# Expert rows stored by slot and gathered by token onto x in SBUF, in place of scatters that add to a copy of x in DRAM

## The reference

```python
# experts are chosen by the token's id; Wg, Wu and Wd are all the context of that expert
def _L0_xattn_ref(hidden_states, token_ids, Wg, Wu, Wd):
    expert_ids = jnp.minimum(tid // tokens_per_expert, E - 1)
    for e in range(E):
        g = jax.nn.silu(jnp.einsum('bsd,fd->bsf', hidden_states, Wg[e]))
        u = jnp.einsum('bsd,fd->bsf', hidden_states, Wu[e])
        y = jnp.einsum('bsf,df->bsd', g * u, Wd[e])
        out = jnp.where((expert_ids == e)[..., None], y, out)
...
x = x + jnp.tanh(g_xattn[0]) * _L0_xattn_ref(_layernorm(x, axis=-1), itok_BxS_13_99985, ctx_2048, ctx_2048, ctx_2048)
x = x + jnp.tanh(g_ffn[0]) * _L0_ffn_ref(_layernorm(x, axis=-1), L0_ffn_w_gate, L0_ffn_w_up, L0_ffn_w_down)
x = x + jnp.tanh(g_xattn[1]) * _L1_xattn_ref(_layernorm(x, axis=-1), ctx_2048, ctx_2048, L1_xattn_gamma)
x = x + jnp.tanh(g_ffn[1]) * _L1_ffn_ref(_layernorm(x, axis=-1), L1_ffn_gate_w, ...)
```

## Time and profile before

| | before |
|---|---|
| median of 3 runs | 1050.43 us (1050.4 to 1052.26) |
| the profiled execution's own time | 1051.51 us |
| its span, first to last instruction | 1049.8 us |
| TensorE busy | 973.2 us, 93% |
| VectorE busy | 632.5 us, 60% |
| ScalarE busy | 420.8 us, 40% |
| GpSimd busy | 639.8 us, 61% |
| mean granted clock of TensorE | 0.979 |

### The profile page before, as it was taken

How to read it: one execution, slowest core, us unless ns; L and a number is a source line. 1 busy time by engine, 2 the same in 40 slices (tenths; PEclk the granted TensorE clock), 3 DMA queues, 4 the chain that set the end, 5 groups by cost and what they waited for, 6 DMA issues and landing times.

```text
span 1049.8 us, 13677 instructions
## 1 busy us (share of the span) xinstructions
PE 973.2 (93%) x4436; PEld 474.9 (45%) x4436; DVE 632.5 (60%) x1168; ACT 420.8 (40%) x817; POOL 639.8 (61%) x565
## 2 busy tenths in 40 slices
PE   6699999969999999799999999999999999999992
PEld 4355555424444444344444445335455555555530
DVE  5478876868888887577777777981222222222221
ACT  4466565434444444466666665332111111111100
POOL 4399996558888887686766661245444554445430
PEclk9899999989999999899999999999999999999996
DMA  9555555240000001230001605178999999999848
GB/s 310 190 131 142 122 144 115 48 143 1 1 1 1 2 1 41 81 130 21 21 23 36 234 1 201 30 259 272 331 336 333 340 335 335 338 335 334 242 63 182
DMA packets 64148, 162.90 MB, mean 155 GB/s; under 512 B 9888, under 2 KB 10032, under 8 KB 63632
## 3 DMA queue, kind: packets, MB, share of 16 engines
q1 hardware_dynamic: 47488, 116.94, 31.9%
q0 software_dynamic: 16464, 40.91, 18.1%
q10 hardware_dynamic: 128, 4.19, 1.2%
HBM read 129.67 MB, written 39.67 MB: 161 GB/s over the span
## 4 chain that ended last, share of the span: by engine, by line
PE 64%; POOL 14%; DVE 8%; issue 7%; DMA 4%; ACT 2%; SPq 0%; POOLq 0%; DVEq 0%; ACTq 0%
PE PS L1580 15%; PE PS L1599 8%; PE PS L1424 6%; PE PS L1401 6%; PE PS L1412 6%; POOL ARENA L665 6%; PE PS L1311 5%; PE PS L1295 5%; POOL ARENA L671 3%; PE PS L1569 3%; PE PS L367 3%; DVE ARENA L986 2%; POOL ARENA L660 1%; DMA XNT<-in_L_ffn_w_down 1%; DVE ARENA L1195 1%
## 5 line engine op out<-in xcount | busy, mean ns | idle before, releaser
L715 POOL TENSOR_TENSOR ARENA<-ARENA 128x512 f32<-128x512 f32 x128 | 133.3, 1063 | 55.8 <-DVE ARENA L1021 55.7
L1366 PE MATMUL PS<-SLAB,ARENA 128*128 128x512 bf16 x512 | 118.8, 382 | 12.6 <-DVE ARENA L972 10.9
L761 POOL DMA_INDIRECT out<-ARENA,idx x32 | 46.2, 1445 | 124.4 <-DVE ARENA L1227 106.8
L1855 ACT ACTIVATE ARENA<-PS 96x192 f32<-96x192 f32 x64 | 20.9, 327 | 226.4 <-PE PS L1580 186.3
L1227 DVE COPY ARENA<-PS 96x512 f32<-96x512 f32 x64 | 41.1, 682 | 94.6 <-PE PS L1599 94.6
L1762 ACT ACTIVATE ARENA<-PS,ARENA 128x512 f32<-128x512 f32 x128 | 86.8, 683 | 23.1 <-DVE ARENA L1015 19.8
L1015 DVE TENSOR_REDUCE ARENA<-PS 128x2 f32<-128x1024 f32 x64 | 78.2, 1222 | 9.3 <-PE PS L1401 9.1
L1366 PEld LDWEIGHTS PS<-SLAB,ARENA 128*128 128x128 bf16 x512 | 48.4, 98 | 75.0 <-issue 21.5
L1580 PE MATMUL PS<-SLAB,ARENA 128*96 128x384 f32 x240 | 81.0, 490 | 0.0
L1412 PEld LDWEIGHTS PS<-ident,ARENA 128*128 128x128 f32 x512 | 54.8, 141 | 51.1 <-issue 36.6
L1728 ACT ACTIVATE ARENA<-PS 128x512 f32<-128x512 f32 x64 | 38.2, 597 | 97.5 <-PE PS L1366 97.5
(11 more groups left out here) (267 smaller groups left out, 1868.3 us busy)
## 6 DMA issues: line engine op xcount, KB each, us to landing
SLAB<-in_L_ffn_w_gate SPq DMA_DIRECT2D x30, 384.0 KB
SLAB<-in_L_ffn_w_up SPq DMA_DIRECT2D x30, 384.0 KB
X<-in_L_ffn_w_down SPq DMA_DIRECT2D x14, 768.0 KB
SLAB<-in_L_ffn_w_down SPq DMA_DIRECT2D x10, 768.0 KB
CT<-in_L_ffn_w_gate SPq DMA_DIRECT2D x16, 384.0 KB
CT<-in_L_ffn_w_up SPq DMA_DIRECT2D x16, 384.0 KB
X<-in_ctx SPq DMA_DIRECT2D x4, 1024.0 KB, 5.5
XNT<-in_L_ffn_w_gate SPq DMA_DIRECT2D x16, 256.0 KB
```

Source lines behind the costliest of these rows:

```text
L715: last = pool.tensor_tensor(prob[s % 4][:, h, :], prob[s % 4][:, h, :], rec[:, s % 4, h:h + 1].to_broadcast([P, D]), ALU.mult)
L1366: last = pe.matmul(bank(b), QT[:, par, k * P:(k + 1) * P], w[:, k, c * D:(c + 1) * D], start=(k == 0), stop=(k == KD - 1))
```

## The change

- The copy `x_sum` is gone, with its four DMAs, the scatters, `target` and `pads`. SP stores each slot's `ysb` to `slot_out` in DRAM, in slot order.
- SP loads x into `X` in SBUF with eight DMAs of two tiles each, in slots 1 to 8.
- When all 19 stores have landed, GpSimd gathers for each token tile i the rows of `slot_out` by `slot[:, i]`, and the DMA adds them to `X` (`gather_x`). Four stand ahead of `deviation_x(0, 1)`, one ahead of `normal_h(0)`, one ahead of `normal_h(1)`, and the other ten in pairs at the end of GpSimd's steps 0 to 4 of the feed-forward.
- `TILED` leaves out slots 6, 12 and 18, and holds all 16 tiles; `REST` is empty. The 15 `unread` multiplications of the passage become 12, in one piece behind y(18).

```diff
         def tile_at(j):
-            return j - (j + 1) // 4
-        TILED = [j for j in range(SLOTS) if j % 4 != 3]
+            return j - j // 6
+        TILED = [j for j in range(SLOTS) if j % 6 or j == 0]
...
+                def store_y(j):
+                    sp.wait_ge(y_out, j + 1)
+                    sp.dma_start(slot_out_v[:, j, :], ysb[:, j % 2, :]).then_inc(y_stored[j % 2], 16)
+
                 for j in range(SLOTS):
                     if j in TILED and tile_at(j) + 2 < NT:
                         load_w(tile_at(j) + 2)
-                sp.wait_ge(y_stored[0], 16 * ((SLOTS + 1) // 2))
-                sp.wait_ge(y_stored[1], 16 * (SLOTS // 2))
-                for i in range(NT):
-                    need(sp, yg_in[i % 4], 16 * (i // 4))
-                    sp.dma_start(X[:, i, :], x_sum_v[:, i, :]).then_inc(yg_in[i % 4], 16)
+                    if 1 <= j <= NT // 2:
+                        need(sp, c_turned, NT)
+                        sp.dma_start(X[:, 2 * j - 2:2 * j, :], x_v[:, 2 * j - 2:2 * j, :]).then_inc(x_in, 16)
+                    if j:
+                        store_y(j - 1)
+                store_y(SLOTS - 1)
...
-                def scatter(j):
-                    if j == 0:
-                        pool.wait_ge(target_ready, 1)
-                        pool.wait_ge(x_in, 64)
-                    pool.wait_ge(y_out, j + 1)
-                    pool.indirect_dma_start(x_sum, bass.IndirectOffsetOnAxis(ap=target[:, j:j + 1], axis=0),
-                                            ysb[:, j % 2, :], None, compute_op=ALU.add).then_inc(y_stored[j % 2], 16)
...
+                def gather_x(i):
+                    need(pool, yg_in[i % 4], 16 * (i // 4))
+                    pool.indirect_dma_start(X[:, i, :], None, slot_out, bass.IndirectOffsetOnAxis(ap=slot[:, i:i + 1], axis=0),
+                                            compute_op=ALU.add).then_inc(yg_in[i % 4], 16)
+
+                pool.wait_ge(x_in, 16 * (NT // 2))
+                pool.wait_ge(y_stored[0], 16 * ((SLOTS + 1) // 2))
+                pool.wait_ge(y_stored[1], 16 * (SLOTS // 2))
+                for i in range(4):
+                    gather_x(i)
                 deviation_x(0, 1)
                 deviation_x(1, 1)
+                gather_x(4)
                 normal_h(0)
                 back_h(0, 0)
                 deviation_x(2, 2)
+                gather_x(5)
                 normal_h(1)
...
                     if live(i, 0):
                         back_i(i, 0, par)
                         normal_i(i, 1, par)
+                    for g in range(2 * i + 6, min(2 * i + 8, NT)):
+                        gather_x(g)
...
-                unread(4)
                 if SLOTS - 1 in TILED:
                     turn_w(tile_at(SLOTS - 1))
-                unread(5)
                 for n in REST:
                     turn_w(n)
-                unread(6)
+                unread(12)
...
-                for b in range(B):
-                    act.dma_start(x_sum[b * S:(b + 1) * S, :], x_rows[b * S:(b + 1) * S, :]).then_inc(x_in, 16)
```

More of the change, by code:

```diff
@@ L102, in build @@
     slot_in = nc.dram_tensor("slot_in", [SLOTS * P, D], F32, kind="Internal").ap()
-    x_sum = nc.dram_tensor("x_sum", [T + SLOTS * P, D], F32, kind="Internal").ap()
+    slot_out = nc.dram_tensor("slot_out", [SLOTS * P, D], F32, kind="Internal").ap()
     rows = nc.dram_tensor("rows", [ROWS, RW], F32, kind="Internal").ap()
@@ L170, in build @@
         hot_ready, counted = sem("hot_ready"), sem("counted")
-        whose_ready, picks_ready, found, token_ready, target_ready = (
-            sem(n) for n in ("whose_ready", "picks_ready", "found", "token_ready", "target_ready"))
+        whose_ready, picks_ready, found, token_ready = (
+            sem(n) for n in ("whose_ready", "picks_ready", "found", "token_ready"))
         h_in = [sem(f"h_in{r}") for r in range(5)]
@@ L202, in build @@
         token = arena(SLOTS, I32)
-        target = arena(SLOTS, I32)
-        pads = arena(2 * SLOTS).rearrange("p (n j) -> p n j", n=2)
         idi = arena(P, I32)
@@ L236, in build @@
         x_rows = x.rearrange("b s d -> (b s) d")
-        x_sum_v = x_sum[0:T, :].rearrange("(i p) d -> p i d", p=P)
+        slot_out_v = slot_out.rearrange("(j p) d -> p j d", p=P)
         def blocks(a, n=BLK):
@@ L629, in _ @@
                         deviation(j + 3)
-                    if j == SLOTS - 1:
-                        scatter(j - 1)
-                    if j in TILED:
+                    if j in TILED and tile_at(j) + 1 < NT:
                         normal(tile_at(j) + 1)
-                    if 0 < j < SLOTS - 1:
-                        scatter(j - 1)
                     if j + HR < SLOTS:
@@ L639, in _ @@
                     normal(n)
-                scatter(SLOTS - 1)
                 def deviation_x(i, n):
@@ L858, in _ @@
                                          op0=ALU.mult, op1=ALU.add).then_inc(token_ready, 1)
[L860 to L865, removed]
                 def top(n):
@@ L925, in _ @@
                     if j in TILED:
-                        scales(n + 1)
+                        if n + 1 < NT:
+                            scales(n + 1)
                         if n + 2 < NT:
@@ L1273, in _ @@
                 for i in range(NT):
-                    last = pe.matmul(bank(3)[:, 0:3 * SLOTS], at_row[:, i, :], picks[:, i].rearrange("p n j -> p (n j)"),
+                    last = pe.matmul(bank(3)[:, 0:2 * SLOTS], at_row[:, i, :], picks[:, i, 0:2].rearrange("p n j -> p (n j)"),
                                      start=(i == 0), stop=(i == NT - 1))
```

## The result

The changed kernel takes **1059.32 us** (median of 4 runs, 1057.37 to 1060.23), beside 1051.35 us for the kernel before (4 runs, 1050.4 to 1052.29). The ratio is 1.0065, with an interval of 1.0052 to 1.0079: slower, by some 8 us in the medians. Six later runs of the same kernel gave 1057.66 beside 1052.72 us, 4.9 us slower (last experiment).

The account below looks back on a forecast made before the run. TensorE was taken to bound the slots, GpSimd and VectorE in turns the feed-forward. -10.2 + 0.2 + 0 + 14.5 = +4.5 on 1051.5 us gave 1056.0, less 1.1 for the median: 1055; range 1043 to 1063.

Parts of the forecast that it names:

- Start of the slots: First layer's early slots: without the copy the weight tile lands in time, z(3) begins at 46.6, not 56.78: -10.2 us.
- Two more turned tiles: Slots 2 to 16: 13 turn a tile in place of 11, 2 x 0.08 = +0.2 us.
- loads of x at nothing: Slots 1 to 8: eight 512 KB loads on SP, each behind its weight tile, cost 0.
- VectorE holds the pace of five tiles in a row: Slots: VectorE's pushes stand 8.45 us apart without a wait, TensorE's slot is 8.47, so VectorE keeps up.
- So it does not delay that tile: Slots 1 to 8: each load of x queues behind its weight tile on SP, so that tile is not delayed.
- Passage, 0: From y(18) to the feed-forward's first transposition: store, four gathers and landing total 19.5 us, 0 against before.
- The term for the tiles taken out of the passage: Passage: moving its two turned tiles into slots gains 0, as TensorE only has fillers in their place.
- The unknown price: GpSimd's cost of a gather that adds, shown in no row: taken as 1.66 us, other end 1.03.
- Feed-forward, +14.5: Steps 0 to 4: ten gathers on GpSimd add 13.2 us, or 15.7 if L986 holds the first; middle taken.
- "held" and "not held": Feed-forward: whether L986 holds each step's first gather, 0.5 us more per step: 15.7 us if so, 13.2 if not.
- Rival 2: Feed-forward: TensorE's clock falls after idling over 3 us at each late L671, +7.5 us: 1062; chance 0.15.
- I took 1.1 us off: Whole kernel: the median of the runs, 1050.43, lay 1.1 below the profiled execution, so 1056.0 became 1055.

Follow-up runs that it names:

- last experiment: The changed kernel run once more, unaltered, six runs: 1057.66 us, ratio 1.0042 to the kernel before.
- the tiles alone: Kernel before with only the new choice of slots for weight tiles and the twelve fillers in one piece; copy and scatters stay: 1050.23 us, ratio 0.9992.
- The second profile: Profiled execution of the unaltered changed kernel's six later runs (median 1057.66 us), the slowest of the six, span 1059.1 us.
- token-order kernel: Against the changed kernel: plain scatters by token to a DRAM tensor in the slots, four direct adding DMAs in the passage, no gathers: 1044.51 us, ratio 0.9918.

## Why the prediction came out as it did

The direction was right, and so was the reason: the copy's stall goes, and GpSimd, which has no time to spare in the feed-forward, gives back more. The size was too small, 1055 forecast against 1059.3; the range held it. By its own steps:

- **Start of the slots, -10.2.** Measured -10.5 (56.62 to 46.09), and 10.6 or 12.2 in the medians when the copy alone is put back. z(3) was forecast for 46.6. Right.
- **Two more turned tiles, +0.2, and loads of x at nothing.** From z(3) to the end of y(18) it takes 1.75 us longer in the first profile (141.39 to 143.14) and 0.8 in the second. Two steps of the prediction are in question. That VectorE holds the pace of five tiles in a row is not borne out: with the tiles alone (no load of x, but the scatters still on GpSimd) two slots take 9.26 and 8.94 us and the stretch 142.9. "So it does not delay that tile" looked at the order on the one queue; without the loads of x the two slots take 8.47 again. Which share each has was not parted. Small in the whole, and above the 0.2 that the forecast allows.
- **Passage, 0 (19.5 us after y(18)).** Measured 19.7, and partly by luck, since the terms were wrong and cancelled. The store landed in 2.0 us and not 3.0, though from its landing to the first gather it then takes 0.8 us and not the 0.4 that the sum has in wake-ups; the four gathers and their gaps take 7.25 us and not 7.5; and the fourth lands 4.2 us after its issue and not 3.1, which was the least of the rows. The term for the tiles taken out of the passage, 0, was wrong as well: in the old kernel they are worth 3.6 us there (19.5 to 15.9). Against the kernel with the tiles alone, the passage with the store and the gathers is so 3.8 us longer. The Trainium skill's estimate of 2.6 us for a DMA of 256 KB from GpSimd ("DMA: Bandwidth & Descriptors", section "Anatomy of one DMA") lies below the adding gather's 3.6. A plain gather lands 2.5 us after its issue (3.5 less 0.99), which agrees with it.
- **The unknown price, 1.66 against 1.03.** The choice by kind and not by direction was right: 1.57 with the add, 0.99 without. It decided the sign: with plain gathers the same program takes 1049.6.
- **Between the first transposition and step 0, nothing was forecast.** It takes 10.8 us in place of 10.1, and lies between 10.1 and 11.7 in the profiles here. The table shows that all of the spread is in the first 32 products: the rest of the stretch is 1.7 us in every row. TensorE is at 0.50 as they begin, and at 1.00 before they end; at 214 to 215 us the granted clock is 0.80 in the changed kernel and still 0.50 with x loaded later.

```profile
218.90 8.38 PE L1366 MATMUL PS<-SLAB,ARENA 128*128 128x512 bf16 x32 [0.78 <-ACT ARENA L1723]
...
210.32 9.07 PE L1363 MATMUL PS<-SLAB,ARENA 128*128 128x512 bf16 x32 [0.78 <-ACT ARENA L1718]
...
209.45 9.98 PE L1364 MATMUL PS<-SLAB,ARENA 128*128 128x512 bf16 x32 [0.78 <-ACT ARENA L1719]
```

These are the kernel before, the changed one and the one with x loaded later. Of the 1.4 us that the last gains in the slots, 0.9 are lost here.
- **Feed-forward, +14.5 (13.2 to 15.7).** Measured +13.0. A short step got +1.8 and one with deviation_x +2.8 where the first gather was not held, against 2.0 and 3.1 at 1.66 us; with 1.57, two gathers are 0.2 us less, and the terms agree to 0.1. The middle that I took between "held" and "not held" was half right: it is held in two steps of five in one execution, in three in the other, and each such step costs some 0.45 us more. The rule of the Trainium skill ("SBUF — State Buffer", section "Who interferes with whom") that whichever of the two issues first makes the other wait is borne out on one side only, and what is measured decides. A L985 that starts 0.11 to 0.14 us ahead does hold the gather (2.03 to 2.11 us); but a gather that is ahead never holds the L985 (0.69 or 0.70 in each step), and being ahead does not always save it. With x loaded later, the first gather of step 1 is 1.06 us ahead, and takes 1.83 us:

```profile
244.37 1.83 POOL L668 DMA_INDIRECT X<-slot_out,slot  x1 [0.17 <-issue]
245.43 0.69 DVE L986 TENSOR_SCALAR ARENA<-ARENA 128x1024 fp8e4<-128x1024 f32 x1
```

It would have ended at 245.94, in the middle of that L986, and ends at 246.20, 0.08 after it; the second gather of step 4 there (291.87) takes 1.92 in the same way. So it is the overlap with the L985 at the gather's beginning or end that costs, and not the order alone; a L985 that begins 0.11 us into a gather and is over well before its end costs nothing (steps 2 and 4 of the changed kernel). This is read from the starts and ends in four profiles; no experiment took L985 away.
- **Rival 2, the clock in the feed-forward.** It does fall a little: 0.96 and 0.93 in the first two steps, 0.97 over the five, where it was 1.00. TensorE's wait before the last transpositions is there, as the rival says (2.70 to 3.56 us in the five steps, 0.19 before), but GpSimd's work sets the step, and the sum agrees without a term for the clock. The second profile shows it best: a step at a granted 0.86 takes 16.15 us, its like at 1.00 in the first profile 16.1.
- **From the profile to the median.** I took 1.1 us off because the median before lay below the profiled execution. With one more run it did not (1051.35 beside 1051.51). And the other three executions of the changed kernel are 2 us and more above the profiled one. The three parts of the miss are so 1.3 in the sum (+5.8 in place of +4.5), 1.1 by that subtraction, and 2.0 by which the median of the changed kernel lies above its profile. The last is mostly a matter of which four runs one has: the six that were run later have their median 0.3 above that profile. Two places are known in which executions differ, z(0) at the lower clock (1.7 us, in three of the seven profiles without the copy) and the 32 products (8.83 to 9.98 in those seven). In the kernel before, the wait for the weight tile covers the first in part: the changed kernel with the copy put back has a z(0) of 5.39 as well, its z(2) begins 2.15 us later than in the kernel before and its z(3) 1.1 later. That the kernel before therefore varies less is not shown: its 33 runs lie between 1049.9 and 1055.14, the ten of the changed kernel between 1055.88 and 1060.87, 5 us wide each.

## What to carry to other kernels

Taking away a transfer that delays a critical load can be worth 10 us of the kernel's time although no compute engine works on it; but look at what takes its place, and on which engine. An indirect DMA is work of its issuer, and an engine that has 1.85 us to spare in a 13 us step (0.77 and 1.08 here) pays for all that goes beyond it. A part of the change that makes no difference in the whole may still be two differences that cancel, so read its stretches too. Where rows must be both sorted and added, do the sorting with plain scatters in a stage where GpSimd waits anyway, and the adding with a few large direct DMAs. And when a forecast hangs on an operation that the trace does not have, choose the nearest row by kind (adding or not) before you choose it by direction (gather or scatter), and say what the sum is by either.

## What the runs showed of the hardware that I had not expected

- **The add has its price twice.** A gather of 128 rows of 2 KB takes 1.57 us of GpSimd with it against 0.99 without, and from start to landing 5.2 against 3.5.
- **A direct adding DMA costs its issuer hardly more for more rows:** 1.35 and 1.77 us for the two with 256 rows, 1.37 for 512 and 1.66 for 1024; the landing is 6.0 and 8.1, 9.0 and 14.4 us.
- **One dip of the clock at a fixed place, in some executions only.** z(0) takes 3.70 or 5.39 us behind the same idle time of 0.77, at a granted clock of 1.00 or 0.66 (25 to 30 us). It begins at 24.2 to 25.0 us in the ones and at 24.8 to 24.9 in the others, so its start does not tell them apart. A single profile does not show which of the two the median has.
- **The same 1.7 us appears in the slots** of the token-order kernel, behind a wait of 2.38 us: y takes 5.39 in place of 3.69, at a granted 0.68. That wait of TensorE cost 1.7 times its length.
- **GpSimd's issue of an indirect DMA and a VectorE cast disturb each other one way only, in these profiles.** The gather gets up to 0.54 us longer, the cast stays at 0.69 or 0.70 us.
